# Causal attention with 16 heads: the probabilities are turned by VectorE in 32x32 blocks instead of by TensorE, the value product runs on 32x64 tiles, and the rope halves are swapped by transfers

## The chip, the cores and the metric

One NeuronCore of a Trainium2 chip runs the program. It has five engines with an instruction stream of their own: TensorE (PE in the rows; its weight loads are PEld), VectorE (DVE), ScalarE (ACT), GpSimd (POOL) and SyncE (SP), which here issues every transfer. They meet only in semaphores. The metric is the device time of one execution in microseconds.

## What is computed

A transformer layer for 4 sequences of 1024 tokens of width 256: layer norm, attention, residual, layer norm, a mixture of experts, residual. The change is in the attention.

```python
q = x @ Wqa @ Wqb                      # 16 heads of 128 + 64 (rope)
compressed, k_pe = split(x @ Wkva)     # 64 + 64
k_nope, v = split(compressed @ Wkvb)   # 128 + 128 for each head
scores = (q_nope @ k_nope.T + rope(q_pe) @ rope(k_pe).T) / sqrt(192)
attn = softmax(where(causal, scores, -max))
x = x + concat_heads(attn @ v) @ Wout
```

## The kernel before

The kernel works with absorbed weights: per head a query row of 128 numbers (64 rope, 64 against the latent) is multiplied with a key row of 128 numbers that all heads share, and the value of a key is its latent row of 64 numbers, in `v32`. Products that need accuracy are made of a high part and a low part (`qh`, `ql`, `kTh`, `kTl`, type fp32r) in three matmuls. The value product is plain fp32, which the trace shows as two loads and two matmuls for each.

`attention_prepare` (the first 70 us) makes keys, values and weights; `attention` runs 8 pairs of heads for each of 4 sequences, 32 pairs; `ffn` follows. The attention is a software pipeline: `run(r)` writes body r, from r = -1 to 32. Body 0 is the first with scores, bodies 1 to 31 are alike, and body 32 (`LAST`) holds only the end of pair 31 and the first steps of the router. The order inside a body is written out by hand in one list for each engine (`TENSOR`, `VECTOR`, `SCALAR`, `POOL`), with lists of their own for body 0 and body 32. In the names c is the half of the queries (0: tokens 0 to 511, 1: 512 to 1023), a the head of the pair, j the tile of 128 queries:

- `Q(c,a)`: queries of a half, two matmuls of 512 columns into a bank of PSUM. `ROT` on VectorE multiplies them with cosine (128 partitions) and, crosswise, with sine (two instructions of 32 partitions) into `rot1` and `rot2`; `ADD` on GpSimd adds; `HIGH` on ScalarE and `LOW` on GpSimd split the sum into `qh` and `ql`.
- `S(c,a,j)`: scores of 128 queries against 128(4c+j+1) keys. `MAX` on VectorE adds the mask and finds the maximum; `EXP` on ScalarE writes the probabilities and their sum. A pair has 16 of each, 9216 columns in all.
- `T(c,kb,a)`: the probabilities of key block kb are turned by TensorE, 128x128 for each query tile (line 1233; 72 for a pair), into three banks of PSUM. `OUT` copies them to `pT`, on ScalarE (line 1318) or VectorE (line 1382).
- `PV(c,first,count)`: value product, `v32` (128 keys x 64) against `pT`, the two heads in the two column halves of the array, 128x64 tiles; three of them for a pair: (1,0,4), (1,4,4), (0,0,4), with 48 matmul records in all.
- `INV`: reciprocals of the row sums; SyncE stores them (line 1107) and reads them back spread over partitions (line 1111) into `linv_b`. `O` on VectorE scales the product with them (line 1400); `OHIGH` (ScalarE) and `OLOW` (GpSimd) split it; `Y` multiplies with the output weights; `ACC` adds into `acc`, which starts as x and is stored per half after 8 pairs.

GpSimd also splits the first expert weights near the end (`split_first_quad`).

## Time and profile before

| | us |
|---|---|
| median of 3 runs | 1732.66 (1731.46 to 1732.78) |
| profiled execution | 1732.48, of which span 1730.7 |
| prepare and body 0 | to about 105 |
| bodies 1 to 31 | 31 of 35.53 each |
| body 32 | 1206.7 to 1238.9 |
| experts | from 1238.9 to the end |

A view by stretches gives busy time of each engine; a list of groups gives the mean length of an instruction, which for TensorE is longer than the distance to the next one, since its matmuls are pipelined. What a matmul costs is therefore read from the starts in the view by time.

### The profile page before, as it was taken

The numbers are of one execution on the slowest core, as the hardware profiler recorded it, in microseconds if no ns is written. First come the engines' busy times: TensorE is split into PE (matmuls) and PEld (weight loads), VectorE is DVE, ScalarE is ACT, GpSimd is POOL, SyncE is SP. The second block draws the span as 40 slices with busy tenths as digits, with TensorE's granted clock in tenths as the row PEclk, the third lists the DMA queues.
The fourth block names the chain that finished last, engine by engine and source line by source line (L and its number), as shares of the span: only waits on it lengthen the run. The fifth ranks groups of instructions, "written<-read, shape, count | busy, mean of one in ns | idle before, by whom it ended". The sixth has DMA issues, their size and how long they took to land.

```text
span 1730.7 us, 31809 instructions
## 1 busy us (share of the span) xinstructions
PE 1662.5 (96%) x11024; PEld 1357.5 (78%) x11024; DVE 1248.5 (72%) x2923; ACT 955.1 (55%) x2255; POOL 509.9 (29%) x433
## 2 busy tenths in 40 slices
PE   5799999999999999999999999999999999999998
PEld 4667777777777777777777777777699999999998
DVE  6888888888888788888888888888654554555543
ACT  6566666666666666666666666666433333433332
POOL 4543334323333333423343333335310110110100
PEclk9899999999999999999999999999999999999999
DMA  8300010012000003000002210001300000000000
GB/s 287 117 26 20 20 32 25 20 47 96 20 25 20 20 32 111 26 20 26 25 26 65 65 32 24 22 19 38 110 1 25 26 1 25 26 14 12 13 13 13
DMA packets 50204, 68.49 MB, mean 40 GB/s; under 512 B 8512, under 2 KB 33088, under 8 KB 50048
## 3 DMA queue, kind: packets, MB, share of 16 engines
q1 hardware_dynamic: 50048, 66.45, 11.6%
q8 instruction: 93, 1.52, 0.4%
q14 instruction: 63, 0.52, 0.1%
HBM read 52.00 MB, written 14.42 MB: 38 GB/s over the span
## 4 chain that ended last, share of the span: by engine, by line
PE 81%; issue 8%; DVE 4%; ACT 2%; DMA 1%; POOL 1%; ACTq 0%; DVEq 0%
PE aps L43 46%; PE fps L43 23%; PE aps L1233 9%; PE fps L1618 2%; ACT probs L1307 1%; DVE f_stats L739 1%; DMA raw_down<-in_down 1%; DVE nmax L1357 0%; POOL rot L1454 0%; PE fps L700 0%; PE fps L668 0%; DVE aTl L1759 0%; DVE rot L1371 0%; DVE aps L1357 0%; DVE rot L792 0%
## 5 line engine op out<-in xcount | busy, mean ns | idle before, releaser
L1307 ACT ACTIVATE probs<-aps,nmax 128x384 f32<-128x384 f32 (+7 forms) x512 | 378.6, 743 | 229.7 <-DVE nmax L1357 224.0
L1357 DVE CUSTOM_DVE_ANT_0 aps<-aps,mask_row 128x384 f32<-128x384 f32 (+7 forms) x512 | 387.2, 772 | 105.9 <-PE aps L43 100.3
L1233 PE MATMUL aps<-ident,probs 128*128 128x128 f32 x2304 | 324.0, 272 | 0.9 <-ACT probs L1307 0.6
L43 PE MATMUL aps<-kTh,qh 128*128 128x512 f32 (+3 forms) x768 | 293.3, 382 | 23.3 <-ACT probs L1307 18.4
L1233 PEld LDWEIGHTS aps<-ident,probs 128*128 128x128 f32 x2304 | 271.7, 140 | 27.2 <-issue 1.5
L1318 ACT COPY pT<-aps 128x512 f32<-128x512 f32 (+3 forms) x485 | 229.5, 504 | 92.1 <-PE aps L1233 89.5
L43 PE MATMUL aps<-pT,v 128*64 128x512 f32 (+3 forms) x1536 | 268.9, 492 | 0.6 <-ACT pT L1318 0.6
L43 PE MATMUL aps<-kTl,qh 128*128 128x512 f32 (+3 forms) x768 | 257.9, 343 | 0.0
L1454 POOL TENSOR_TENSOR rot<-rot 64x512 f32<-64x512 f32 x128 | 163.9, 1280 | 211.8 <-DVE rot L1371 211.8
L43 PE MATMUL aps<-kTh,ql 128*128 128x512 f32 (+3 forms) x768 | 221.8, 343 | 0.0
L43 PEld LDWEIGHTS aps<-pT,v 128*64 128x64 f32 x1536 | 101.7, 136 | 152.1 <-issue 142.1
L1461 POOL TENSOR_TENSOR ql<-rot,qh 128x512 fp32r<-128x512 f32 x128 | 164.9, 1288 | 158.5 <-ACT qh L1299 158.5
L43 PEld LDWEIGHTS aps<-kTh,qh 128*128 128x128 f32 x768 | 145.7, 190 | 74.4 <-issue 57.9
L1468 POOL TENSOR_TENSOR ol<-o,oh 128x512 fp32r<-128x512 f32 x64 | 82.3, 1286 | 352.8 <-ACT oh L1325 352.8
L1702 ACT CAST aTh<-fps 128x512 fp32r<-128x512 f32 (+1 forms) x96 | 52.9, 552 | 236.1 <-PE fps L1618 236.0
L1759 DVE TENSOR_TENSOR aTl<-fps,aTh 128x512 fp32r<-128x512 f32 (+1 forms) x96 | 62.0, 647 | 167.3 <-ACT aTh L1702 167.3
L43 PE MATMUL fps<-wth,qh 128*128 128x352 f32 x512 | 176.1, 344 | 2.0 <-PEq L833 2.0
L1371 DVE TENSOR_TENSOR rot<-aps,sinT 32x512 f32<-32x512 f32 x256 | 174.2, 680 | 3.5
L43 PE MATMUL fps<-wtl,qh 128*128 128x352 f32 x512 | 166.3, 325 | 0.0
L43 PE MATMUL fps<-wth,ql 128*128 128x352 f32 x512 | 166.2, 325 | 0.0
L43 PEld LDWEIGHTS aps<-kTl,qh 128*128 128x128 f32 x768 | 146.7, 191 | 9.5
L43 PEld LDWEIGHTS aps<-kTh,ql 128*128 128x128 f32 x768 | 136.7, 190 | 8.2
(190 smaller groups left out, 2878.1 us busy)
## 6 DMA issues: line engine op xcount, KB each, us to landing
linv_b<-inverses_scratch SPq DMA_DIRECT2D x128, 128.0 KB, 2.8
wqs<-wq_scratch SPq DMA_DIRECT2D x30, 256.0 KB, 3.1
raw_numbers<-in_x SPq DMA_DIRECT2D x8, 512.0 KB, 6.2
acc<-in_x SPq DMA_DIRECT2D x8, 512.0 KB, 4.0
inverses_scratch<-linv_t SPq DMA_DIRECT2D x256, 1.0 KB
x_scratch<-acc SPq DMA_DIRECT2D x8, 512.0 KB, 2.9
x<-x_scratch SPq DMA_DIRECT2D x8, 512.0 KB, 3.9
out<-x SPq DMA_DIRECT2D x7, 512.0 KB, 2.9
```

The lines of the kernel that those rows point to most:

```text
L43: return nc.tensor.matmul(out, lhsT, rhs, start=start, stop=stop, skip_group_check=True)
L1233: last = nc.tensor.transpose(tps[:, TS.index(x) % 3, j * P:(j + 1) * P], probs[c][:, c * (pair % 2), a, off:off + P], t.ident[:])
L1307: nc.scalar.activation(probs[c][:, c * (r % 2), a, off:off + w], sps[:, at:at + w], ACT.Exp, bias=nmax[:, c, a, j:j + 1], scale=-1.0, accu ...
L1318: nc.scalar.copy(pT[:, k % PT_BUFS, s:QC], tps[:, k % 3, s:QC]).then_inc(t_sb["scalar"], 1)
L1357: nc.vector.tensor_tensor_reduce(out=s, in0=s, in1=mask[:, N - PW[c][j]:N], scale=-1.0, scalar=3.0e38, op0=ALU.add, op1=ALU.min, accum_out ...
L1371: last = nc.vector.tensor_tensor(rot2[to:to + 32, k, :], sps[source:source + 32, at:at + QC], t.sinT[to:to + 32, cols], ALU.mult)
L1454: nc.gpsimd.tensor_tensor(rot1[0:64, k, :], rot1[0:64, k, :], rot2[:, k, :], ALU.add).then_inc(q_add, 1)
L1461: nc.gpsimd.tensor_tensor(ql[:, a, cols], rot1[:, k, :], qh[:, a, cols].bitcast(F32), ALU.subtract).then_inc(q_split, 1)
L1468: nc.gpsimd.tensor_tensor(ol[:, cols], o32[:, c, :], oh[:, cols].bitcast(F32), ALU.subtract).then_inc(o_low, 1)
L1618: last = nc.tensor.transpose(turned_in(i, q)[:, (m - 4 * q) * P:(m - 4 * q + 1) * P], act_sb[:, i % 2, m * P:(m + 1) * P], t.ident[:])
L1702: nc.scalar.copy(aTh[:, i % 2, m.start:m.stop, :].rearrange("p m n -> p (m n)"), turned_in(i, q)[:, 0:len(m) * P]).then_inc(aT_h, 1)
L1759: nc.vector.tensor_tensor(aTl[:, i % 2, m.start:m.stop, :].rearrange("p m n -> p (m n)"), turned_in(i, q)[:, 0:len(m) * P], aTh[:, i % 2, ...
```

## The change

- `T` and `OUT` go. `TURN(c,a,j)` on VectorE turns the whole probability row block of one `EXP` in blocks of 32x32, SBUF to SBUF: on partitions 32a' to 32a'+31 lie then, for each block b of 32 keys, the probabilities of those keys for the queries 32a' to 32a'+31 of every query tile. There are 16 for a pair, 128 to 1024 columns wide, one for each `EXP`. `EXP` writes into a ring of 5 rows, so it waits for the `TURN` of 5 rows before.
- The value product contracts 32 keys at a time: for each block b, each row group a' and each head a matmul of 32 rows x 64 columns, at most 128 columns moving, into banks 4 to 7 (one for each row group). A pair has 244 + 116 = 360 of them, with two passes each 720 records in the place of 48. They are written as six pieces of eight key blocks. Values lie four times over partitions in `vrep`, loaded by SyncE in pieces of 256 bytes.
- `ROT` on VectorE becomes: `RAW`, one copy of PSUM to `rot1` by ScalarE; `SWAP`, two transfers of 32 partitions that swap the halves into `rot2`; and three instructions on GpSimd, sine product, cosine product, sum.
- `acc` is double, loaded and stored for a whole sequence at once. `vrep` of sequences 0 and 1 is loaded at the end of body 0. Storing and spreading the inverses are two jobs of SyncE's list. The first expert weights are split by ScalarE and VectorE in body 32.
- All order lists and bank numbers are new.

```diff
-                    for j in range(t_cols(x) // P, 4):
-                        last = nc.tensor.transpose(tps[:, TS.index(x) % 3, j * P:(j + 1) * P],
-                                                   probs[c][:, c * (pair % 2), a, off:off + P], t.ident[:])
-                            last = mm(nc, ops[64 * a:64 * a + 64, s:QC], t.v32[:, pair // PAIRS % 2, kb, :],
-                                      pT[:, k % PT_BUFS, s:QC], kb == 0, kb == KB[c] - 1)
+                    if part == 0:
...
+                        pe.wait_ge(p_turned, last_of("tr", c, pair))
+                        banks_free(x)
+                    n = BLOCKS[c] // PARTS[c]
+                    for b in range(part * n, (part + 1) * n):
+                        for a in range(4):
+                            s = max(0, b // 4 - 4 * c) * S32
+                            if b // 4 >= 4 * c and b % 4 > a:
+                                s += S32
+                            if s == 4 * S32:
+                                continue
+                            for h in range(2):
+                                last = mm(nc, banks[64 * h:64 * h + 64, OB + a, s:4 * S32],
+                                          vrep[32 * a:32 * a + 32, pair // PAIRS % 2, b, :],
+                                          pT[c][32 * a:32 * a + 32, h, b, s:], b == 0, b == BLOCKS[c] - 1)
...
+                def turn_job(x):
+                    dve.wait_ge(e_done, count(EXP(c, a, j), r))
+                    if r > 0:
+                        dve.wait_ge(pv_done, last_of("p", c, r - 1))
+                    nc.vector.transpose(pT[c][:, a, 0:w // S32, j * S32:(j + 1) * S32],
+                                        probs[:, SLOT[EXP(c, a, j), r], 0:w].rearrange("p (b k) -> p b k", k=S32))\
+                        .then_inc(p_turned, 1)
...
-                    nc.vector.tensor_tensor(rot1[:, k, :], sps[:, at:at + QC], t.cosT[:, cols], ALU.mult)
-                    for to, source in ((0, 32), (32, 0)):
-                        last = nc.vector.tensor_tensor(rot2[to:to + 32, k, :], sps[source:source + 32, at:at + QC],
-                                                       t.sinT[to:to + 32, cols], ALU.mult)
+                    nc.scalar.copy(rot1[:, rot_slot(x, r), :], banks[:, bank_of(Q(c, a), r), :]).then_inc(q_raw, 1)
...
+                sp.dma_start(rot2[0:32, k, :], rot1[32:64, k, :]).then_inc(q_swapped[k], 16)
+                sp.dma_start(rot2[32:64, k, :], rot1[0:32, k, :]).then_inc(q_swapped[k], 16)
...
+                    nc.gpsimd.tensor_tensor(rot2[:, k, :], rot2[:, k, :], t.sinT[:, cols], ALU.mult).then_inc(q_turned, 1)
+                    nc.gpsimd.tensor_tensor(rot1[0:64, k, :], rot1[0:64, k, :], t.cosT[0:64, cols], ALU.mult)\
+                        .then_inc(q_turned, 1)
+                    pool.wait_ge(q_turned, 2 * n)
                     nc.gpsimd.tensor_tensor(rot1[0:64, k, :], rot1[0:64, k, :], rot2[:, k, :], ALU.add).then_inc(q_add, 1)
```

TensorE, in a body of the middle, the second half of the value product of c = 1 before (`PV(1,4,4)`, a piece between scores and transposes):

```order
L1233 MATMUL aps<-ident,probs 128x128 x2
L43 MATMUL aps<-pT,v 64x512 [waits pT_by_vector_in_sbuf,pT_by_scalar_in_sbuf]
L43 MATMUL aps<-pT,v 64x512
L43 MATMUL aps<-pT,v 64x384 x2
L43 MATMUL aps<-pT,v 64x256 x2
L43 MATMUL aps<-pT,v 64x128 x2
L43 MATMUL aps<-kTh,qh 128x384 [waits exp_done,q_split]
```

and after, the last of its four pieces (`PV(1,3)`), with the output product that follows:

```order
L46 MATMUL aps<-pT_second,vrep 64x64 x8
L46 MATMUL aps<-pT_second,vrep 64x32 x2
L46 MATMUL aps<-pT_second,vrep 64x64 x6
L46 MATMUL aps<-pT_second,vrep 64x32 x4
L46 MATMUL aps<-pT_second,vrep 64x64 x4
L46 MATMUL aps<-pT_second,vrep 64x32 x6
L46 MATMUL aps<-pT_second,vrep 64x64 x2
L46 MATMUL aps<-pT_second,vrep 64x32 x20
L46 MATMUL aps<-w2h,oh 128x256 [waits exp_done,o_low]
```

One matmul of the list is a load and a matmul for each of two passes. The transposes between the pieces are gone, and each piece is many short matmuls.

VectorE, the middle of a body, before (the four `ROT` of a pair stand between the maxima):

```order
L1369 TENSOR_TENSOR rot<-aps,cosT 128x512 [waits q_split,q_ps]
L1371 TENSOR_TENSOR rot<-aps,sinT 32x512 x2
L1357 ISA aps,nmax<-aps,mask_row 128x896 [waits scores_ready]
L1357 ISA nmax 128x1
L1369 TENSOR_TENSOR rot<-aps,cosT 128x512 [waits q_split,q_ps]
L1371 TENSOR_TENSOR rot<-aps,sinT 32x512 x2
L1382 COPY pT<-aps 128x384 [waits pv_done,pT_ready]
L1382 COPY pT<-aps 128x256 [waits pv_done,pT_ready]
```

and after, where `O(1)` opens the turns of the second half:

```order
L1406 STREAM_TRANSPOSE pT_first<-probs 128x8x32 [waits pv_done,exp_done]
L1428 TENSOR_TENSOR o32<-aps,linv_b 128x4x4x32 [waits o_low,inverses_1_in_sbuf,pv_done]
L1406 STREAM_TRANSPOSE pT_second<-probs 128x28x32 [waits pv_done,exp_done]
L1440 TENSOR_TENSOR acc<-aps,acc 128x512 [waits y_ps,x_even_loaded]
L1396 ISA aps,nmax<-aps,mask_row 128x896 [waits scores_ready]
L1396 ISA nmax 128x1
L1396 ISA aps,nmax<-aps,mask_row 128x768 [waits scores_ready]
```

The turn reads `probs` and no PSUM, and stands behind `O(1)` because both need the value product of the pair before to be done.

SyncE, a body of the middle, before:

```order
L1114 DMA wqs<-wq_scratch 128x512 [waits q_ps]
L1107 DMA inverses_scratch<-linv_t 8x32 [waits inverses_turned,o_in_sbuf]
L1107 DMA inverses_scratch<-linv_t 8x32 x3
L1111 DMA linv_b<-inverses_scratch 64x512 [waits inverses_0_kept]
L1111 DMA linv_b<-inverses_scratch 64x512
```

and after:

```order
L1146 DMA wqs<-wq_scratch 128x512 [waits q_ps]
L1142 DMA rot<-rot 32x512 [waits q_raw]
L1143 DMA rot<-rot 32x512
L1130 DMA inverses_scratch<-linv_t 8x32 [waits inverses_turned,o_in_sbuf]
L1130 DMA inverses_scratch<-linv_t 8x32 x3
L1142 DMA rot<-rot 32x512 [waits q_raw]
L1143 DMA rot<-rot 32x512
L1137 DMA linv_b<-inverses_scratch 64x512 [waits inverses_1_kept]
```

The swap of the second head's queries now stands behind the wait for the inverses of the pair.

## Rows read from the trace of the kernel before

**Rows 1.** The page: busy time, share of the span and instructions of each engine.

```profile
PE 1662.5 (96%) x11024; PEld 1357.5 (78%) x11024; DVE 1248.5 (72%) x2923; ACT 955.1 (55%) x2255; POOL 509.9 (29%) x433
```

**Rows 2.** Stretches: length, busy of PE, PEld, DVE, ACT, POOL, PEclk, DMA; a middle body, body 32.

```profile
595.32:630.85 35.53, 34.77 (x224) 26.69 (x225) 29.18 (x64) 22.66 (x54) 12.76 (x10) 1.00 0.07 24
1206.70:1238.90 32.20, 28.71 (x212) 21.63 (x210) 21.84 (x58) 15.70 (x31) 16.98 (x14) 0.95 0.41 133
```

**Rows 3.** Chain of waits in order of time: start, length, what (eight transposes).

```profile
567.32 0.87 PE aps L1233 x8
```

**Rows 4.** PE by time (start, length, instruction): both shapes of value product and what follows.

```profile
587.66 2.37 PE L43 MATMUL aps<-pT,v 128*64 128x512 f32 x16
589.97 0.44 PE L43 MATMUL aps<-kTh,qh 128*128 128x384 f32 x1
...
1215.66 3.65 PE L43 MATMUL aps<-pT,v 128*64 128x512 f32 x16
1219.24 1.95 PE L1233 MATMUL aps<-ident,probs 128*128 128x128 f32 x15
```

**Rows 5.** PE by time, the router and mask products on 32-row and 32-column tiles.

```profile
1238.87 0.43 PE L43 MATMUL fps<-mw,xq 32*128 32x352 f32 x4
1239.23 0.50 PE L43 MATMUL fps<-wth,mu 128*32 128x352 f32 x4
...
1240.44 0.78 PE L43 MATMUL fps<-wth,mu 128*32 128x352 f32 x8
1241.03 0.78 PE L43 MATMUL fps<-wtl,mu 128*32 128x352 f32 x8
```

**Rows 6.** DMA queues: the one that carries TensorE's instructions.

```profile
q8 instruction: 93, 1.52, 0.4%
```

**Rows 7.** DVE groups: instruction, out<-in, shapes, count, busy, mean ns, idle before.

```profile
L1371 DVE TENSOR_TENSOR rot<-aps,sinT 32x512 f32<-32x512 f32 x256 | 174.2, 680 | 3.5
L1369 DVE TENSOR_TENSOR rot<-aps,cosT 128x512 f32<-128x512 f32 x128 | 87.0, 680 | 10.1 <-PE aps L43 8.5 <-POOL ql L1461 1.3 <-issue 0.2
L789 DVE COPY rot<-soft_h 128x512 f32<-128x512 f32 x8 | 3.4, 427 | 0.3
```

**Rows 8.** Tile pT: its copies by VectorE, ns shortest, median, longest.

```profile
L1382 DVE COPY pT<-aps x283: 280/552/691, 90.2 to 1201.7; 128x256 f32<-128x256 f32 x49, 128x384 f32<-128x384 f32 x45, 128x512 f32<-128x512 f32 x33, 128x128 f32<-128x128 f32 x15
```

**Rows 9.** DVE by time: a 32x32 turn, the maximum behind it, and two maxima.

```profile
579.24 0.21 DVE L1392 STREAM_TRANSPOSE linv_t<-linv 128x32 f32<-128x32 f32 x1
579.38 0.65 DVE L1369 TENSOR_TENSOR rot<-aps,cosT 128x512 f32<-128x512 f32 x1
...
586.55 1.23 DVE L1357 CUSTOM_DVE_ANT_0 aps<-aps,mask_row 128x1024 f32<-128x1024 f32 x1
587.70 0.14 DVE L1357 DVE_READ_ACCUMULATOR2_ANT nmax<- 128x1 f32 x1
```

**Rows 10.** ACT and POOL groups: copies of the turned blocks, rope sum, low part.

```profile
L1318 ACT COPY pT<-aps 128x512 f32<-128x512 f32 (+3 forms) x485 | 229.5, 504 | 92.1 <-PE aps L1233 89.5
L1454 POOL TENSOR_TENSOR rot<-rot 64x512 f32<-64x512 f32 x128 | 163.9, 1280 | 211.8 <-DVE rot L1371 211.8
L1461 POOL TENSOR_TENSOR ql<-rot,qh 128x512 fp32r<-128x512 f32 x128 | 164.9, 1288 | 158.5 <-ACT qh L1299 158.5
```

**Rows 11.** POOL by time: the low part waits for the high part.

```profile
575.07 1.28 POOL L1461 TENSOR_TENSOR ql<-rot,qh 128x512 fp32r<-128x512 f32 x1 [0.73 <-ACT qh L1299]
```

**Rows 12.** DMA issues: out<-in, count, KB each, us from issue to landing.

```profile
linv_b<-inverses_scratch SPq DMA_DIRECT2D x128, 128.0 KB, 2.8
v<-values_scratch SPq DMA_DIRECT2D x2, 256.0 KB, 7.1
```

**Rows 13.** PE by time at the start; the chain of waits at the end of body 32.

```profile
77.55 0.69 PE L43 MATMUL aps<-kTh,qh 128*128 128x384 f32 x1 [4.22 <-POOL ql L1461]
...
1230.70 3.17 DMA x_scratch<-acc
1233.89 8.80 DMA raw_down<-in_down
```

More of the change, by code:

```diff
@@ new lines, in attention @@
+        SCALAR = [RAW(1, 0), RAW(1, 1), EXP(0, 0, 0), EXP(0, 0, 3), EXP(0, 0, 1), EXP(0, 1, 3), HIGH(1, 0),
+                  EXP(0, 1, 0), EXP(0, 0, 2), EXP(0, 1, 2), EXP(0, 1, 1), RAW(0, 0), EXP(1, 0, 0), HIGH(1, 1),
+                  EXP(1, 0, 2), OHIGH(1), RAW(0, 1), EXP(1, 1, 2), EXP(1, 0, 1), EXP(1, 1, 0), HIGH(0, 0),
+                  EXP(1, 0, 3), EXP(1, 1, 1), HIGH(0, 1), EXP(1, 1, 3), OHIGH(0)]
+        POOL = [ROT(1, 0), LOW(1, 0), ROT(1, 1), LOW(1, 1), ROT(0, 0), OLOW(1), LOW(0, 0), ROT(0, 1), LOW(0, 1),
+                OLOW(0)]
@@ new lines, in attention, with of @@
+        SS = [x for x in TENSOR if x[0] == "s"]
+        COUNT, KINDS = {}, {}
+        for bodies in (tensor_body, vector_body, scalar_body, pool_body, sync_body):
+            for r in BODIES:
+                for x in bodies(r):
+                    if x[0] not in ("router", "mask", "stats", "quad"):
+                        KINDS[x[0]] = KINDS.get(x[0], 0) + 1
+                        COUNT[x, r] = KINDS[x[0]]
+        def count(x, r):
+            return COUNT[x, r]
+        def of(kind, x):
+            return (kind,) + x[1:]
@@ L1295, in high_job @@
                     pair = r + age(x)
[L1296 removed]
+                    act.wait_ge(q_add, count(ROT(c, a), r))
                     if pair > 0:
[L1298 to L1299 removed]
+                        act.wait_ge(s_ready, max(at_pair(y, pair - 1) for y in SS if y[1:3] == (c, a)))
```

603 lines of the change are left out of this document (293 added, 310 removed).

## The prediction

> **What bounds the kernel now.** I read the page first: TensorE is busy 96% of the span, VectorE 72% [rows 1]. Then one body of the middle, since 31 equal bodies of 35.53 us make 1101 of the 1730.7 us: there TensorE is busy 34.77 us, VectorE 29.18, ScalarE 22.66, GpSimd 12.76 [rows 2]. TensorE leaves 0.76 us free, so a pair costs what TensorE's list costs. The question is what the list costs after the change, and which other list is then the longest.
>
> **TensorE, what goes.** Eight transposes take 0.87 us on the chain, 0.109 each [rows 3]; 72 for a pair make 7.8 us. The value products go in their old form: two pieces of the narrowing kind (512, 384, 256 and 128 columns) take 589.97 - 587.66 = 2.31 us each, the piece with 512 columns throughout 1219.24 - 1215.66 = 3.58 [rows 4], together 8.2. What stays (scores, queries, output product, small gaps) is 34.77 - 7.8 - 8.2 = 18.8 us.
>
> **TensorE, what comes.** From the two pieces the rate of today: 2 passes of 1280 columns take 2.31 us, 2 passes of 2048 take 3.58; the difference, 1536 column passes in 1.27 us, is 0.83 ns each, and 0.18 us is left over per piece for entering and leaving the tiled form. A pair streams 4608 columns for each row group (the fourth row group has the most), at two passes 9216 x 0.83 = 7.7 us if all eight tiles (four row groups, two column halves) run side by side. Where only 32 columns move, the load of 64 weight columns is longer: a load of 128 columns is hidden in 0.109 us [rows 3], so I take 0.055 for 64 against 0.027 for the stream, 16 times, 0.4 us. Six pieces at 0.18 make 1.1. Sum 9.2 us. TensorE's new list: 18.8 + 9.2 = 28.0 us.
>
> Do eight tiles run side by side? The row-tiled form is in the trace: four matmuls of 32 rows and 352 columns begin together and the next instruction starts 1239.23 - 1238.87 = 0.36 us later, their loads, the stream and a change of form included [rows 5]. One after the other, four streams of 352 columns at the 0.83 ns of fp32 or even half of that would take 0.58 us or more without the loads. Column tiles too: eight matmuls of 352 columns in four column tiles follow each other in 0.59 us [rows 5], that is 0.295 for four, the same 0.83 ns a column. The two together are not in the trace, nor is a stretch with so many starts. Bound from below: 9.2. From above: today's narrowest value matmuls start two in every 0.109 us; if no faster rate of starts existed, 720 x 0.055 = 39 us. I take 9.2, because within a group of four the starts cost nothing that the 0.36 us leave room for.
>
> The Trainium skill, "TensorEngine Tiling (Array Packing)", Performance Considerations, Instruction Overhead, speaks against the change: it gives each matmul about 60 cycles of overhead and warns against tiling a dimension that is small already. At 2.4 GHz that is 25 ns, and 720 of them are an estimate of 18 us instead of 9.2 by that page. The four starts in rows 5 don't bear it out as a cost in series. It would lead to the second rival.
>
> TensorE's instructions come in packets: 93 of them for the 11,024 matmuls, as many loads [rows 1] and the waits between, some 250 instructions each; they take 0.4% of 16 engines' 1730.7 us, 1.2 us each [rows 6]. A body will have about 1700 instructions, 6.6 packets, 8 us in 30. I cost it at nothing; its cover is the work before a piece, and without it one packet, 1.2 us, would show in each piece of 256 instructions, 7 us a pair.
>
> **VectorE.** `ROT` goes: (174.2 + 87.0) / 32 = 8.2 us a pair [rows 7]. Its copies go: 283 of about 0.5 us, 4.4 us a pair [rows 8]. 29.2 - 8.2 - 4.4 = 16.6 us stay (maxima, sums, scaling, inverses). 16 turns of 9216 columns come. A turn of 32 columns lasts 0.21 us and the next instruction starts after 0.14 [rows 9]. VectorE's rate elsewhere is near 1.04 ns a column: the maximum of 1024 columns gives way after 1.15 us [rows 9]. Wide turns are not in the trace. From below: at the rate of the copy inside SBUF, 427 ns for 512 columns [rows 7], 9216 x 0.83 = 7.7 us. From above: if all of the 0.21 us for 32 columns beyond the 0.14 of spacing were per-column work, 2.2 ns, 20 us. I take 1.04 ns and 0.15 us an instruction, 9.6 + 2.4 = 12.0, since 32 columns at 1.04 ns leave 0.11 to 0.18 us of fixed cost, as everywhere on this engine. VectorE's new list: 28.6 us, now the longest by a little.
>
> **ScalarE** loses 229.5 / 32 = 7.2 us of copies and gains four of about 0.59, 2.4 [rows 10]: 17.9 us, no bound. **GpSimd**: for each of four query tiles three instructions of 1.28 and one of 1.29, and `OLOW` twice 1.29: 23.1 us [rows 10]; `LOW` waits 0.73 us for `HIGH` [rows 11], 2.9 for four, 26.0 in all. It starts after `RAW` (0.6) and a swap; the nearest transfer lands in 2.8 us [rows 12]. The first chain in a body is 0.5 + 0.6 + 2.8 + 3.8 + 0.7 + 1.3 = 9.7 us, and TensorE reaches the first scores of the second half after some 9 us of other work. The second swap waits in SyncE's queue behind the wait for the inverses, whose instruction on VectorE comes after about 4 us; GpSimd is then still busy with the first until 9.7. So the wait is hidden; uncovered it would cost 2.8 us a pair.
>
> **Period.** Three lists of 28.6 (VectorE), 28.0 (TensorE) and 26.0 us (GpSimd). The first piece of the value product waits for all turns of its half, and these turns wait for the last piece of the pair before: about 16 us of VectorE (eight turns of 8.3, six maxima, the sums) and 11 us of TensorE (6.9 of pieces, 4.3 of scores and queries between) in turn, 27 us, inside 28.6. Today the bound engine leaves 0.76 us; with a second list as long I take 1.2: 29.8 us. 31 x (35.53 - 29.8) = 178 us saved.
>
> **Ends.** Body 0 waits for GpSimd today (4.22 us once [rows 13]) and will wait for its three instructions and the swap; the values are loaded only at its end, 7.1 us for such a load [rows 12]. Nothing to 10 us, I take +5. Body 32 (32.2 us) loses 52 transposes, 5.7 us, but VectorE gets 3.7 us of weight splitting ahead of `O(1)`, and the store before the load of the expert weights doubles from 512 KB in 3.17 us [rows 13]: from -5 to +4, I take 0. The experts are untouched. Sum on the profiled execution: span 1730.7 - 178 + 5 = 1558, and 1.8 around it, 1560. The runs' median is 0.2 us from the profiled execution.
>
> **Rivals.**
> 1. The queries bound a body. For: GpSimd's 26.0 us are close, and two of the four swaps stand behind waits in SyncE's list. If both are uncovered with their `RAW`, 26.0 + 2 x 3.4 = 32.8, with gaps 33.2 us: 1730.7 - 72 + 5 + 1.8 = 1665. Against: two slots of `rot1` let a swap run while GpSimd works on the other.
> 2. Slower: the eight tiles take turns. If the row groups go in two turns, the pieces cost 16.2 + 1.1 us, TensorE's list is 36.1, the period 37.5: 1730.7 + 61 + 5 + 1.8 = 1799. It decides from 22 ns a matmul on (720 of them in 15.7 us, where TensorE's list reaches 35.5). For: no stretch of the trace has so many starts, and 39 us is the far bound. Against: rows 5. The page named above would give 18 us and a period near 39, about 1845.
> 3. Slower: turns at 2.1 ns a column, 21.6 us, VectorE's list 38.2, the period 39: 1845. Against: the 0.14 us spacing of the narrow turn. It decides from 19 us of turns on.
>
> **How the numbers follow.** The forecast (period 28.3 to 32, 1513 to 1630) has 0.68, rival 1 0.14, rival 2 0.11, rival 3 0.05, and 0.02 lie at no change. Predicted 1560. From 1495 (turns at the copy's rate, TensorE's list alone) to 1690 leaves out rivals 2 and 3. A difference of 0.2% is about what a measurement can tell from none; faster by more than that 0.82, within it 0.02, slower 0.16.
>
> **What would show it.** A middle body near 30 us with VectorE busy above 27; a 1024-wide turn giving way after about 1.2 us; a full piece of 128 matmuls in 1.9 us with eight starts within 0.06 us; the low part of the second half's queries done before TensorE asks. A piece above 2.8 us makes rival 2 true, a turn above 2 us rival 3, TensorE waiting for `ql` rival 1.

## The result

The changed kernel takes 1748.38 us (median of 6 runs, 1743.20 to 1754.92), the kernel before 1732.72 (6 runs, 1731.46 to 1733.13): 1.0094 times as long, with a 95% interval of 1.0069 to 1.0119. It is slower by 16 us where 173 us less were forecast (1560), and it lies outside the range of 1495 to 1690. Its runs also differ among themselves by 0.7%, those of before by 0.1%. The profiled execution took 1750.21 us, its span 1748.4.

The page of the profile after, answering to [rows 1] and [rows 6]: busy time of TensorE and VectorE, the granted clock in 40 slices, the queue that brings TensorE's instructions, the chain by engine.

```profile
PE 1564.5 (89%) x30224; PEld 1355.7 (78%) x30224; DVE 1185.9 (68%) x2772; ACT 810.9 (46%) x1902; POOL 819.2 (47%) x681
...
PEclk9889999998999999899999899999899999999999
...
q8 instruction: 240, 3.93, 0.9%
...
PE 70%; DVE 7%; issue 6%; DMA 5%; POOL 4%; ACT 2%; SPq 2%; DVEq 0%; ACTq 0%; POOLq 0%
```

TensorE is busy 98 us less than before, yet the span is 18 us longer: a gain is there and is given back as idle time. The packets of instructions went from 93 to 240. The chain has 6% "issue", time in which nothing that the profile shows was waited for. That share alone is no sign of anything new, since the chain of the kernel before has more of it:

```profile
PE 81%; issue 8%; DVE 4%; ACT 2%; DMA 1%; POOL 1%; ACTq 0%; DVEq 0%
```

What is new is a wait for issue in front of TensorE's matmuls, in the list of waits below.

Stretches from one first-half reciprocal of VectorE (L1416) to the next, one per body: length, busy of PE, PEld, DVE, ACT, POOL, PEclk, DMA. The first two are bodies of the middle, the third stands at the end of the first sequence, the last is the first body.

```profile
460.10:492.50 32.40, 30.59 (x844) 25.78 (x834) 26.98 (x60) 17.98 (x42) 20.55 (x17) 1.00 0.14 37
492.50:527.40 34.90, 30.97 (x844) 25.89 (x835) 27.27 (x60) 18.09 (x42) 23.89 (x20) 1.00 0.17 48
378.60:425.70 47.10, 32.97 (x794) 27.87 (x787) 27.37 (x59) 18.12 (x42) 22.52 (x19) 0.86 0.49 131
95.67:140.40 44.73, 30.82 (x652) 25.53 (x651) 26.30 (x58) 17.98 (x42) 20.97 (x18) 0.81 0.64 123
```

ScalarE does what was forecast (18 us), and VectorE is busy 27 us where its list was put at 28.6. TensorE leaves 1.8 us of the shorter body and 3.9 of the longer one idle, so no engine fills its body. From the times of the same reciprocals, the whole span:

| us | before | after | e5_spread_early | e6_spread_early_quarter |
|---|---|---|---|---|
| start to the first reciprocal | 89.8 | 95.7 | 96.3 | 96.3 |
| first body | 27.1 | 44.7 | 35.3 | 28.9 |
| three bodies at sequence ends | 35.5 each | 47.1, 47.3, 43.4 | 33.3, 33.9, 34.3 | 30.6, 29.9, 30.1 |
| the 27 others, mean | 35.55 | 34.09 | 33.77 | 30.22 |
| rest of the last body and experts | 547.4 | 549.8 | 550.6 | 545.0 |

The last two columns are experiments told below. Before, the 27 bodies lie between 35.5 and 35.8; after, between 31.2 and 37.7.

Three kinds of idle time stand behind this. First, TensorE by time: start, length, instruction, and in brackets the idle time before it. A whole piece of the value product, and one that stops after 108 of its 128 matmuls.

```profile
586.85 2.10 PE L46 MATMUL aps<-pT_second,vrep 32*64 32x128 f32 x128
588.88 0.33 PE L46 MATMUL aps<-kTh,qh 128*128 128x128 f32 x1
...
449.62 1.84 PE L46 MATMUL aps<-pT_second,vrep 32*64 32x128 f32 x108
452.91 0.65 PE L46 MATMUL aps<-pT_second,vrep 32*64 32x128 f32 x20 [1.45 <-issue]
```

The whole piece gives way after 588.88 - 586.85 = 2.03 us (forecast 1.9): eight tiles do run side by side. The other one waits in its middle, where no semaphore stands. Behind such a stop the granted clock can fall to the lower of its two levels:

```profile
562.43 1.44 PE L46 MATMUL aps<-pT_second,vrep 32*64 32x64 f32 x104
563.81 0.39 PE L46 MATMUL aps<-w2h,oh 128*128 128x256 f32 x1
...
574.86 0.43 PE L46 MATMUL aps<-pT_first,vrep 32*64 32x96 f32 x17 [2.24 <-issue]
...
577.03 2.15 PE L46 MATMUL aps<-pT_first,vrep 32*64 32x64 f32 x104
579.11 0.58 PE L46 MATMUL aps<-w2h,oh 128*128 128x256 f32 x1
```

The granted clock is 1.00 from 562.43 to 563.81 and 0.50 (1.2 GHz) from 576.6 to 583.2; two pieces of 104 matmuls give way after 1.38 and 2.08 us.

Second, SyncE at the end of the first sequence (start, time in which it issues, transfer), and GpSimd at the same place.

```profile
392.05 8.35 SPq L1156 DMA_DIRECT2D vrep<-values_scratch  x4
403.83 0.38 SPq L1211 DMA_DIRECT2D x_scratch<-acc  x1
408.41 0.39 SPq L1160 DMA_DIRECT2D acc<-in_x  x1
...
409.72 0.54 SPq L1142 DMA_DIRECT2D rot<-rot  x1
...
416.47 1.25 POOL L1488 TENSOR_TENSOR rot<-rot,sinT 64x512 f32<-64x512 f32 x1 [14.56 <-DMA rot<-rot]
```

The first swap of the next body is issued only after the residual is stored (403.83), has landed (408.41) and 1 MB for a later sequence is asked for; it lands behind that megabyte at 416.47. Third, the waits, total, times and longest:

```profile
PEld aps L46 <- issue: 203.8, 383, 3.4
POOL rot L1488 <- DMA rot<-rot: 192.1, 65, 16.9
...
PE aps L46 <- issue: 89.3, 85, 3.8
...
PE aps L46 <- POOL ql L1498: 35.2, 10, 10.6
...
PE aps L46 <- DMA vrep<-values_scratch: 10.0, 1, 10.0
```

TensorE's 10.0 us for the first values lie in the first body. The same view of the kernel before:

```profile
PEld aps L43 <- issue: 225.2, 714, 3.0
...
PE aps L43 <- issue: 0.6, 1, 0.6
```

Weight loads waited for issue as much before, and they overlap matmuls. The matmuls themselves waited 0.6 us before and wait 89.3 now, in 85 places.

### The profile page after: what moved, and what is told of

The parts are those of the page before. It is cut to its first block, busy times and chain, and to the rows that moved or that the text cites. A ratio compares the mean times of both kernels' runs of the same rounds, so it can differ in the third digit from the quotient of the medians.

```text
span 1748.4 us, 69212 instructions
## 1 busy us (share of the span) xinstructions
PE 1564.5 (89%) x30224; PEld 1355.7 (78%) x30224; DVE 1185.9 (68%) x2772; ACT 810.9 (46%) x1902; POOL 819.2 (47%) x681
## 3 DMA queue, kind: packets, MB, share of 16 engines
q1 hardware_dynamic: 82432, 87.44, 17.6%
## 4 chain that ended last, share of the span: by engine, by line
PE 70%; DVE 7%; issue 6%; DMA 5%; POOL 4%; ACT 2%; SPq 2%; DVEq 0%; ACTq 0%; POOLq 0%
PE aps L46 44%; PE fps L46 23%; DMA rot<-rot 3%; PE fps L1649 2%; DVE aps L1396 2%; DVE pT_second L1406 2%; POOL rot L1492 1%; POOL rot L1488 1%; DVE acc L1440 1%; POOL rot L1489 1%; POOL ql L1498 1%; DMA x_scratch<-acc 1%; ACT probs L1348 1%; SPq L1130 1%; SPq L1142 1%
## 5 line engine op out<-in xcount | busy, mean ns | idle before, releaser
L1348 ACT ACTIVATE probs<-aps,nmax 128x1024 f32<-128x1024 f32 (+7 forms) x512 | 375.8, 738 | 318.4 <-DVE nmax L1396 303.6
L1396 DVE CUSTOM_DVE_ANT_0 aps<-aps,mask_row 128x384 f32<-128x384 f32 (+7 forms) x512 | 379.7, 761 | 188.9 <-PE aps L46 187.4
L46 PE MATMUL aps<-kTh,qh 128*128 128x512 f32 (+3 forms) x768 | 286.4, 373 | 45.8 <-POOL ql L1498 35.2
L46 PEld LDWEIGHTS aps<-pT_second,vrep 32*64 32x64 f32 x15616 | 231.9, 134 | 82.2 <-issue 79.6
L46 PE MATMUL aps<-pT_second,vrep 32*64 32x128 f32 (+1 forms) x15616 | 266.3, 265 | 29.5 <-issue 28.2
L1406 DVE STREAM_TRANSPOSE pT_second<-probs 128x768 f32<-128x768 f32 (+3 forms) x256 | 258.6, 1030 | 1.4 <-ACT probs L1348 0.3
L1488 POOL TENSOR_TENSOR rot<-rot,sinT 64x512 f32<-64x512 f32 x128 | 162.9, 1273 | 192.1 <-DMA rot<-rot 192.1
L46 PE MATMUL aps<-pT_first,vrep 32*64 32x128 f32 (+3 forms) x7424 | 120.7, 249 | 52.7 <-issue 42.5
L46 PEld LDWEIGHTS aps<-pT_first,vrep 32*64 32x64 f32 x7424 | 105.8, 136 | 78.5 <-issue 68.1
L1337 ACT CAST qh<-rot 128x512 fp32r<-128x512 f32 x128 | 79.2, 619 | 183.9 <-POOL rot L1492 183.7
L1489 POOL TENSOR_TENSOR rot<-rot,cosT 64x512 f32<-64x512 f32 x128 | 163.4, 1276 | 0.0
L46 PEld LDWEIGHTS aps<-kTl,qh 128*128 128x128 f32 x768 | 148.3, 193 | 12.2 <-issue 1.7
```

Of the source, the lines that this page charges most:

```text
L46: return nc.tensor.matmul(out, lhsT, rhs, start=start, stop=stop, skip_group_check=True)
L1337: nc.scalar.copy(qh[:, a, c * QC:(c + 1) * QC], rot1[:, rot_slot(x, r), :]).then_inc(q_high, 1)
L1348: nc.scalar.activation(probs[:, SLOT[x, r], 0:w], sps[:, at:at + w], ACT.Exp, bias=nmax[:, c, a, j:j + 1], scale=-1.0, accum_out=lsum[:, c ...
L1396: nc.vector.tensor_tensor_reduce(out=s, in0=s, in1=mask[:, N - PW[c][j]:N], scale=-1.0, scalar=3.0e38, op0=ALU.add, op1=ALU.min, accum_out ...
L1406: nc.vector.transpose(pT[c][:, a, 0:w // S32, j * S32:(j + 1) * S32], probs[:, SLOT[EXP(c, a, j), r], 0:w].rearrange("p (b k) -> p b k", k ...
L1488: nc.gpsimd.tensor_tensor(rot2[:, k, :], rot2[:, k, :], t.sinT[:, cols], ALU.mult).then_inc(q_turned, 1)
```

## The experiments

The theory is that instruction supply, the order of SyncE's list at sequence ends, and the late load of the first values cost the gain, each by itself. The rival is the prediction's first: queries, swaps and GpSimd bound a body.

**e1_boundary.** The transfers of a sequence end go out one or two per body, between the last swap and `KEEP(0)`. With `n = r % 8`, `between` issues the keys at n = 0 to 2, the values at 3 to 6, the stores at 1 to 4 (256 KB each in place of one of 1 MB) and the loads of the residual at 6 and 7 (512 KB each). The router's and the first experts' loads are spread over the last sequence in the same way.

```diff
                 for x in sync_body(r):
+                    if 1 <= r < LAST and x == KEEP(0):
+                        between(r)
                     job[x[0]](x, r)
...
                     sp.dma_start(x2_v[b], acc[:, 1 - b % 2]).then_inc(x2_stored, 16)
-                    if b + 2 < B:
-                        sp.wait_ge(x2_stored, 16 * (b + 1))
-                        load_acc(b + 2)
```

> The order of SyncE's transfers at the three sequence ends alone is changed: keys (3 of 512 KB), values (4 of 256 KB), residual stores (4 of 256 KB) and loads (2 of 512 KB), the router's and the experts' loads go out one per body, behind the last swap of the body, in place of all at once ahead of the next body's first swap. Theory (queue order): bodies 8, 16 and 24, which took 47.1, 47.3 and 43.4 us beside 34.1 of the others, fall to the others' length: 1748.4 - 3 x 12 = 1712 (1705 to 1722). Rival (those bodies are long because of instruction supply or the clock): under 10 us less, 1740 to 1748.

Measured: 1699.84 us (1691.66 to 1705.78), ratio to before 0.9813 [0.9774, 0.9853]; 48 us less than the changed kernel and below the expected 1705 to 1722. The three bodies take 33.2, 32.7 and 34.4 us. The one at the end of the first sequence has its full clock again (0.86 in the changed kernel):

```profile
383.15:416.35 33.20, 30.78 (x806) 25.45 (x792) 27.22 (x59) 18.20 (x42) 19.90 (x17) 1.00 0.18 52
```

These three give 37.5 us (137.8 to 100.3); the others 9.7 (27 times 34.09 - 33.73). This version is faster than both kernels, and it leaves nothing out.

**e2_quarter.** The value product on tiles of 128 rows, a quarter of the instructions.

```diff
-                        for a in range(4):
...
-                            for h in range(2):
-                                last = mm(nc, banks[64 * h:64 * h + 64, OB + a, s:4 * S32],
-                                          vrep[32 * a:32 * a + 32, pair // PAIRS % 2, b, :],
-                                          pT[c][32 * a:32 * a + 32, h, b, s:], b == 0, b == BLOCKS[c] - 1)
+                        s = max(0, b // 4 - 4 * c) * S32
+                        for h in range(2):
+                            last = mm(nc, banks[64 * h:64 * h + 64, OB + b % 4, s:4 * S32],
+                                      vrep[:, pair // PAIRS % 2, b, :], pT[c][:, h, b, s:], b < 4, b >= BLOCKS[c] - 4)
```

> The value product on 128x64 tiles in place of 32x64: a piece has 32 matmuls and 32 weight loads in place of 128 and 128, and about the same columns streamed side by side. It leaves out the parting of the four query groups, so that the weighted values are mixed; everything else is as in the changed kernel. Theory (instruction supply): about 1.3 packets of 256 instructions a body go in place of 6.9 or so, no piece is broken, and a normal body falls from 34.1 to 30 to 31.5 us: 1748 - 27 x 3.1 = 1665 (1640 to 1690). Rival (queries, swaps and GpSimd set the body): the normal body stays at 33 to 34 us, 1720 to 1748.

Measured: 1631.62 us (1626.93 to 1635.50), 0.9421 [0.9402, 0.9441]. The 27 bodies fall from 34.09 to 30.27 us, inside the expected 30 to 31.5; the time is 8 us below the expected range. The sequence ends stay long (44.5, 45.0, 38.3). TensorE's matmuls have no wait for issue left in the attention. The rival is refuted as the main cause: neither queries nor GpSimd were touched.

**e4_noswap.** `SWAP` issues nothing, and GpSimd's first product reads `rot1[0:64]` in place of `rot2`.

```diff
-                sp.dma_start(rot2[0:32, k, :], rot1[32:64, k, :]).then_inc(q_swapped[k], 16)
-                sp.dma_start(rot2[32:64, k, :], rot1[0:32, k, :]).then_inc(q_swapped[k], 16)
```

> The swaps of the rope halves leave out their transfers: GpSimd multiplies the unswapped halves by the sines as soon as ScalarE has copied the queries, so that the queries are wrong; the number of GpSimd's instructions is the same. Rival (the chain ScalarE copy, swap, GpSimd, ql sets the body): each chain is some 3 to 4 us shorter, TensorE's waits for ql (77 us in all) go, 1748 to 1680 or less. Theory (instruction supply and queue order): only what the swap lost behind the transfers at three sequence ends comes back, about 7 us each, 1720 to 1740.

Measured: 1691.56 us (1688.80 to 1692.18), 0.9766 [0.9751, 0.9780], between the two expectations. Sequence ends take 38.7, 40.3 and 39.1, so 20 us of the 57 are theirs; the 27 bodies take 32.85 in place of 34.09, another 33. The rival holds in part; e9 and e10 return to it.

**e6_fine.** The second half's value product in eight pieces of four key blocks, one between every two score or query tiles.

```diff
-PARTS = [2, 4]
+PARTS = [2, 8]
...
-        TENSOR = [Q(1, 0), Q(1, 1), S(0, 0, 2), S(0, 0, 0), S(0, 0, 3), Y(0, 0), S(0, 0, 1), S(0, 1, 3), PV(1, 0),
+        TENSOR = [Q(1, 0), Q(1, 1), S(0, 0, 2), S(0, 0, 0), S(0, 0, 3), Y(0, 0), S(0, 0, 1), PV(1, 0), S(0, 1, 3),
+                  PV(1, 1), S(0, 1, 0), PV(1, 2), S(0, 1, 1), PV(1, 3), S(0, 1, 2), PV(1, 4), S(1, 0, 0), PV(1, 5), Q(0, 0),
+                  PV(1, 6), S(1, 0, 2), PV(1, 7), Q(0, 1), Y(0, 1), S(1, 1, 2), S(1, 0, 1), S(1, 1, 0), S(1, 0, 3),
```

> The value product of the second half in eight pieces of four key blocks (128 instructions each), one between every two score or query tiles, in place of four pieces of eight key blocks (256 instructions); the number of instructions is unchanged and so is every other engine's order. Theory (instruction supply): 6.9 packets of 3.4 us are 23.5 us of a body of 34.1, so they suffice if the instructions are asked for evenly; the four pieces of the second half no longer run out, and a body falls by 1 to 2 us: 1695 to 1725. Rival (the pieces break for another reason, or the query chain sets the body): within 8 us of 1748.

Measured: 1780.59 us (1779.38 to 1782.17), 1.0286 [1.0269, 1.0303], 32 us slower than the changed kernel: a miss. The matmuls' waits for issue fell only from 89.3 to 61.8 us and those of the weight loads rose from 203.8 to 243.4, while VectorE and ScalarE wait longer for scores that now come later:

```profile
PEld aps L46 <- issue: 243.4, 545, 3.6
...
ACT probs L1348 <- DVE nmax L1396: 421.0, 319, 11.2
DVE aps L1396 <- PE aps L46: 275.2, 125, 14.8
```

In the changed kernel the last two are 303.6 and 187.4. The run moved two things at once and doesn't decide between them.

**m1_supply.** TensorE alone. `small(64)` is 64 products on 32x64 tiles with 128 columns, that is 128 loads and 128 matmuls; `long` is products on 128x128 with 512 columns.

```diff
+            for _ in range(12):
+                small(64)
+            long(96)
```

> TensorE alone, with nothing to wait for: 12 pieces of 256 instructions (64 products on 32x64 tiles, 128 columns) in a row; then 10 pieces each followed by 14, 10 or 6 long products (128x128, 512 columns); then 20 half pieces each followed by 7 or 3 long ones. It computes nothing of the reference. Theory (instructions arrive at one packet of 256 per 3.4 us at best): the 12 pieces take 12 x 3.4 = 41 us though one takes 1.7 us uninterrupted; 14 long ones (3.1 us) behind a piece cover it, 4.8 us a round; 6 long ones (1.3 us) don't, 3.6 us a round in place of 3.0; a half piece with 7 long ones isn't held (2.4 us a round), with 3 it is (1.8 in place of 1.5). Rival (the pieces broke because the fetches shared the DMA engines with other transfers, of which there are none here): the 12 pieces take 20 to 22 us and no round is longer than its products.

Measured, TensorE by time, the start of the 12 pieces, the end, a round with six long products, and a half piece with three:

```profile
34.28 3.84 PE L46 MATMUL aps<-x,w 32*64 32x128 f32 x255
39.27 2.08 PE L46 MATMUL aps<-x,w 32*64 32x128 f32 x128 [1.15 <-issue]
42.73 2.08 PE L46 MATMUL aps<-x,w 32*64 32x128 f32 x128 [1.38 <-issue]
...
75.46 0.32 PE L46 MATMUL aps<-x,w 32*64 32x128 f32 x1 [1.37 <-issue]
75.71 22.07 PE L46 MATMUL aps<-xl,wl 128*128 128x512 f32 x96
...
226.05 2.10 PE L46 MATMUL aps<-x,w 32*64 32x128 f32 x128
...
229.66 2.16 PE L46 MATMUL aps<-x,w 32*64 32x128 f32 x128
...
352.61 1.21 PE L46 MATMUL aps<-x,w 32*64 32x128 f32 x64
...
354.64 1.21 PE L46 MATMUL aps<-x,w 32*64 32x128 f32 x64
```

The 12 pieces take 75.71 - 34.28 = 41.4 us, 3.45 each, where their work is 2.03; there are no other transfers. After the first 510 instructions TensorE mostly stops after every 128 matmuls and 128 loads. From that first stop on a piece takes (75.46 - 39.27) / 10 = 3.62 us; the step from 39.27 to 42.73, 3.46 us, is the fastest that repeats. Supply is shown as a limit by itself, at about 13.5 to 14 ns an instruction. The granted clock was at its lower level for 10 of these 41 us, which makes the pieces there longer, but the steps of 3.46 us stand at the full clock. Rounds with 14 and with 10 long products ran without a stop, as did half pieces with seven. The shorter rounds were forecast badly: six long products behind a piece made a round of 3.6 us by their own length, with one stop in ten rounds (268 instructions at 13.4 ns each, just at the limit), and the half pieces with three (2.03 us a round of 134 instructions, 15 ns each) ran without a stop, since they asked for no more than that rate.

The Trainium skill, "Runtime: NRT & Kernel Launch", Instruction fetch mechanics, says that instructions arrive in blocks of 256, the next block while the current one runs, and that crossing a block is mostly hidden. The 256 agree with the packets (70 for the 17,898 loads and matmuls of this run); the last does not hold where 256 instructions run in 2.03 us. The first stop after 510 instructions fits the two blocks in hand of which a note in that section speaks, not the 2048 instructions that the section gives TensorE.

**e3_half.** Both heads' columns in one product on 32x64 tiles, even and odd key blocks on the two halves of the array: half the instructions.

```diff
-                            for h in range(2):
-                                last = mm(nc, banks[64 * h:64 * h + 64, OB + a, s:4 * S32],
...
-                                          pT[c][32 * a:32 * a + 32, h, b, s:], b == 0, b == BLOCKS[c] - 1)
+                            g = b % 2
...
+                            last = mm(nc, banks[64 * g:64 * g + 64, OB + a, 2 * s:8 * S32].rearrange("p (h t) -> p h t", h=2),
+                                      vrep[32 * a:32 * a + 32, pair // PAIRS % 2, b, :],
+                                      pT[c][32 * a:32 * a + 32, :, b, s:], b < 2, b >= BLOCKS[c] - 2)
```

> The value product on 32x64 tiles with both heads' 128 columns in one product of 256 columns, even key blocks on one half of the array and odd ones on the other: half the instructions (128 in place of 256 a piece), about the same columns side by side. It leaves out adding the two halves, so that the output is of no use; everything else is as in the changed kernel. Theory (instruction supply): 3.5 to 4 packets a body in place of 6.9; almost no piece is broken, and the time is near that of the quarter (1631.6): 1635 to 1660. Rival (the small tiles themselves are slow, and the quarter won by its 128-row tiles): above 1700.

Measured: 1633.90 us (1630.68 to 1635.23), 0.9431 [0.9417, 0.9445], the quarter's time within 2.3 us, with 150 packets in place of 108 and 240. So it is the number of instructions and not the 32-row tiles, and half of them is already few enough: the matmuls' waits for issue are 2.1 us.

**e5_spread_early.** e1_boundary, with `load_values(0)` ahead of body 0's swaps and the second sequence's loads in bodies 3 and 4. The lines are against e1_boundary.

```diff
-                if r == 0:
+                if r == -1:
                     sp.wait_ge(t.values_stored, 32)
-                    for b in (0, 1):
-                        load_values(b)
-                        load_acc(b)
+                    load_values(0)
```

> The changed kernel with the sequence transfers one per body, as in e1_boundary, and the first sequence's values loaded ahead of the first body's swaps (they are stored at 70 us and were asked for at 107); the second's values and residual go out in bodies 3 and 4. Theory (queue order): the first body's 10.0 us wait for the values goes as well: 1699.8 - 10 = 1690 (1684 to 1697). Rival (TensorE has something else to wait for there): 1697 to 1702.

Measured: 1700.12 us (1697.33 to 1706.07), 0.9820 [0.9801, 0.9840]. In the profiled executions the first body falls from 43.9 to 35.3 us and the span from 1703.7 to 1695.5, but the medians of the two versions, from runs that spread over 9 and 14 us, don't show it: inconclusive for the time.

**e6_spread_early_quarter.** e5_spread_early and the quarter together, both edits as above.

> e5_spread_early with the value product on 128x64 tiles (a quarter of its instructions; the parting of the four query groups is left out, so that the weighted values are mixed). Theory (queue order, first values and instruction supply are three costs that add up): in e2_quarter the three bodies at sequence ends took 44.5, 45.0 and 38.3 us beside 30; without that excess of 38 us and the first wait of 10 us, 1631.6 - 48 = 1584 (1575 to 1592), and every body near 30 us. Rival (one stall hid the other): above 1600.

Measured: 1577.75 us (1577.06 to 1578.37), 0.9108 [0.9093, 0.9123]. The costs add up: 1700.12 - 1577.75 = 122 us hang on the number of instructions, and the 53.9 us less than e2_quarter on the order of the transfers and the first values. Its output is of no use, so it measures what the costs are worth and is no kernel that could replace the other. The first body falls from 42.6 to 28.9 us, the scatter of the runs is gone (0.1%), and the bodies are level. One of the middle, and one at a sequence end:

```profile
305.86:335.92 30.06, 29.34 (x302) 24.12 (x300) 26.84 (x60) 17.79 (x42) 23.12 (x20) 1.00 0.17 46
366.49:396.33 29.84, 29.28 (x302) 24.10 (x300) 26.72 (x59) 17.79 (x42) 21.51 (x18) 1.00 0.24 66
```

Not all of the 122 us are stops. The same full piece as at 586.85, with a quarter of the instructions:

```profile
327.72 1.97 PE L46 MATMUL aps<-pT_second,vrep 128*64 128x128 f32 x32
329.62 0.33 PE L46 MATMUL aps<-kTh,qh 128*128 128x128 f32 x1
```

It gives way after 1.90 us in place of 2.03, and the pieces with narrower products save more (1.05 in place of 1.38). By the medians of the unbroken pieces at full clock, the six of a pair take 10.7 us on the 32x64 tiles and 9.3 in the quarter. That is some 40 of the 122 us for 32 pairs, an estimate from these lengths. The matmuls' waits for issue are 77.2 us in e5_spread_early and none here; how much of these and of the lower clock behind them shows in the time was not separated.

**e7_even, e8_even_less.** e5_spread_early with TensorE's order alone changed. e7 moves score tiles, queries and output products; e8 moves two output products. e7:

```diff
-        TENSOR = [Q(1, 0), Q(1, 1), S(0, 0, 2), S(0, 0, 0), S(0, 0, 3), Y(0, 0), S(0, 0, 1), S(0, 1, 3), PV(1, 0),
-                  S(0, 1, 0), S(0, 1, 1), S(0, 1, 2), PV(1, 1), S(1, 0, 0), Q(0, 0), PV(1, 2), S(1, 0, 2), Q(0, 1),
-                  PV(1, 3), Y(0, 1), S(1, 1, 2), S(1, 0, 1), S(1, 1, 0), S(1, 0, 3), S(1, 1, 1), PV(0, 0), S(1, 1, 3),
-                  PV(0, 1), Y(1, 1), Y(1, 0)]
+        TENSOR = [Q(1, 0), Q(1, 1), S(0, 0, 2), S(0, 0, 0), S(0, 0, 3), Y(0, 0), S(0, 0, 1), PV(1, 0), S(0, 1, 3),
+                  S(0, 1, 0), S(0, 1, 1), S(0, 1, 2), PV(1, 1), Q(0, 0), S(1, 0, 0), S(1, 0, 2), PV(1, 2), Q(0, 1), Y(0, 1),
+                  S(1, 0, 1), PV(1, 3), S(1, 1, 2), S(1, 1, 0), S(1, 0, 3), S(1, 1, 1), PV(0, 0), S(1, 1, 3), Y(1, 1),
+                  PV(0, 1), Y(1, 0)]
```

> e5_spread_early with TensorE's order of a body changed so that more other work stands between two pieces of 256 instructions: some 1.6 us behind the first of the second half (was 1.0), 2.3 behind the second (1.2), 2.0 behind the third (1.6), 1.9 behind the first of the first half (1.3). Other engines' orders and all counts are unchanged. Theory (a fetch of 256 instructions costs 3.45 us and is only asked for when the one before it has arrived, so that each run of 256 instructions must last 3.45 us by itself): pieces of 1.7 us with 1.8 us behind them fit, the breaks in pieces (43 over 0.5 us, 54 us in all) fall to less than half, a normal body from 33.8 to 31.5 to 33, 1625 to 1675. Rival (scores that come later hold up VectorE and ScalarE, as in e6_fine): 1695 to 1730.

> As e7_even but only two products of the attention's output are moved: one ahead of the fourth piece of the second half, one between the two pieces of the first half. No score is moved. Theory: two of the four short distances grow by 0.6 us each, 1680 to 1697. Rival (distances don't matter): 1697 to 1703.

Measured: e7 1841.21 us (1838.08 to 1855.81), 1.0647 [1.0620, 1.0674]; e8 1701.94 (1694.46 to 1711.07), 0.9832 [0.9804, 0.9859], no change against e5_spread_early. e7 is a miss by far, outside both of its expectations. In it TensorE waits for exponentials whose banks it needs sooner, and VectorE for value products that come later:

```profile
DVE o L1449 <- PE aps L46: 202.0, 63, 7.3
PE aps L46 <- ACT probs L1369: 119.8, 109, 3.3
```

In e5_spread_early the first is 38.2 and the second 4.2. In e8 the matmuls' waits for issue fell from 77.2 to 56.9 us and VectorE's wait for value products rose from 38.2 to 65.1, so a stop that is taken away does not give its length back by itself. Whether a better spacing could hide the supply is left open; in the two orders tried, moving scores cost more than it brought.

**e9_noswap, e10_shadow.** e5_spread_early without the swaps, and with transfers of the same shape that no engine reads or waits for; SyncE alone sees to it that the last one into the same slot has landed (the line with the plus stands in e10 alone).

```diff
-                sp.dma_start(rot2[0:32, k, :], rot1[32:64, k, :]).then_inc(q_swapped[k], 16)
+                sp.dma_start(shadow[0:32, k, :], t.cosT[32:64, 0:QC]).then_inc(q_swapped[k], 16)
```

> e5_spread_early without the transfers of the rope halves (GpSimd takes the unswapped halves at once, the queries are wrong). Theory (the queries' chain costs the rest of a normal body by itself, 34.09 to 32.85 in e4_noswap): 1700 - 31 x 1.0 = 1665 to 1680. Rival (the swap cost only behind the transfers at sequence ends, which are spread here): 1693 to 1702.

> As e9_noswap, but transfers of the same size and shape still go out at the same places, from a table into a buffer that nobody reads, and nobody waits for them. It tells the traffic from the wait. Theory (the wait for the swap costs, not its traffic): within 4 us of e9_noswap. Rival (the swaps' 64 KB get in the way of the instruction fetches on the same DMA engines): near e5_spread_early, 1693 to 1702.

Measured: e9 1673.10 us (1668.48 to 1677.92), 0.9662 [0.9646, 0.9678]; e10 1690.09 (1683.65 to 1693.51), 0.9756 [0.9740, 0.9771]. Of the 27 us, 17 come back with the traffic alone and 10 hang on the wait. The intervals of e9 and e10 don't meet; those of e10 and e5 do not either, with 0.3% between them. e10 lies between its two expectations, nearer the second.

**m2_traffic.** m1's row of 12 pieces three times: alone, beside swaps, beside 1 MB loads.

```diff
+            for n in range(12):
+                sp.dma_start(to[0:32, 0, :], xl[32:64, :].bitcast(F32)).then_inc(moved, 16)
+                sp.dma_start(to[32:64, 0, :], xl[0:32, :].bitcast(F32)).then_inc(moved, 16)
+                sp.wait_ge(moved, 32 * (n + 1))
...
+            for n in range(5):
+                sp.dma_start(big[:], ins["x"].rearrange("b (t p) d -> b p t d", p=P)[n % 4]).then_inc(moved, 16)
```

> TensorE alone as in m1_supply: three times 12 pieces of 256 instructions in a row, each behind 97 long products. Beside the first nothing moves; beside the second swaps of the rope's shape go out (two of 32x2048 bytes) one after the other; beside the third loads of 1 MB one after the other. It computes nothing of the reference. Theory (fetches share the DMA engines with the transfers): 41.4 us the first time, 43 to 48 beside the swaps, 60 or more beside the 1 MB loads. Rival (fetches are not held by other transfers): 41 to 42 three times.

Measured, TensorE by time, start and end of the three rows of pieces:

```profile
34.89 3.85 PE L46 MATMUL aps<-x,w 32*64 32x128 f32 x254
...
77.41 22.28 PE L46 MATMUL aps<-xl,wl 128*128 128x512 f32 x97
99.62 2.51 PE L46 MATMUL aps<-x,w 32*64 32x128 f32 x157
...
145.86 23.26 PE L46 MATMUL aps<-xl,wl 128*128 128x512 f32 x97
169.05 2.95 PE L46 MATMUL aps<-x,w 32*64 32x128 f32 x188
...
208.18 3.72 PE L46 MATMUL aps<-x,w 32*64 32x128 f32 x128 [4.92 <-issue]
...
223.63 22.28 PE L46 MATMUL aps<-xl,wl 128*128 128x512 f32 x97
```

42.5 us alone, 46.2 beside the swaps, 54.6 beside the loads (which ran for 25 of them, with single stops up to 4.92 us). The stops in the three rows come to 14.7, 17.9 and 22.8 us. The rest of the differences goes with the granted clock, 0.92, 0.91 and 0.81 in the three rows. So transfers do lengthen the supply, the loads less than expected. It is a way in which traffic can cost time that nobody waits for. That it is what cost the 17 us of e10 is not shown: its matmuls wait 73.8 us for issue, those of e9 67.2, and the other 10 us were traced to no wait.

**e11_by_scalar.** e5_spread_early with the swap as two copies by ScalarE.

```diff
+                    nc.scalar.copy(rot2[0:32, k, :], banks[32:64, bank, :])
+                    nc.scalar.copy(rot2[32:64, k, :], banks[0:32, bank, :])
+                    nc.scalar.copy(rot1[:, k, :], banks[:, bank, :]).then_inc(q_raw, 1)
```

> e5_spread_early with the two swaps of a rope half made by ScalarE, which copies 32 rows of the queries from PSUM twice more (32x512, about 0.6 us each by the 0.585 us of its 128x512 copy, 4.7 us a body) in place of the two transfers. Theory (the traffic and the latency of the swaps cost 17 and 10 us, and ScalarE, 18 of 33.8 us busy, has room): 1673 to 1688. Rival (ScalarE's longer turn delays the exponentials or the query banks come free later): 1695 to 1715.

Measured: 1704.35 us (1699.12 to 1715.43), 0.9858 [0.9829, 0.9886], no gain over 0.9820 [0.9801, 0.9840]. ScalarE's busy time grows by 150 us, 4.7 a pair, and what the missing transfers give back is used up; which wait takes it was not isolated.

## Why the prediction was wrong

- **What it had right.** VectorE's turns (1.04 ns a column and 0.15 us) are 1221 ns for 1024 columns and 308 for 128, the measured slope 1.02 ns:

```profile
L1406 DVE STREAM_TRANSPOSE pT_second<-probs 128x1024 f32<-128x1024 f32 x64 | 78.2, 1221 | 0.0
L1406 DVE STREAM_TRANSPOSE pT_first<-probs 128x128 f32<-128x128 f32 x64 | 19.7, 308 | 33.6 <-ACT probs L1348 33.4
```

  The 391 us of all turns are 12.2 a pair (forecast 12.0); rival 3 is refuted. The eight tiles run together, a whole piece in 2.03 us (1.9), so rival 2 is refuted. The Trainium skill, "TensorEngine Tiling (Array Packing)", Performance Considerations, Instruction Overhead, gives about 60 cycles a matmul, and for tiles of this size the trace does not agree: 128 matmuls in 2.03 us are 16 ns each.
- **What was luck.** With the causes taken away the 31 periods average 30.2 us against 29.8, and the kernel takes 1577.75 against 1560. Part of this nearness is luck. It was reached with a quarter of the instructions, whose pieces take 9.3 us a pair; those of the forecast kernel take 10.7 even unbroken, against the 9.2 of the sum. And the engine that fills the body is TensorE, busy 29.3 us (28.0 in the sum), not VectorE, busy 26.8 (28.6): two errors of opposite sign.
- **The step that failed: packets "I cost it at nothing".** The text had the count right (6.6 a body) and the size of one, and even a price if uncovered (7 us a pair). It took the work before a piece as cover, because it asked whether 6.6 packets of 1.2 us fit into 30 us on the DMA engines. The question was how fast one can follow another: 3.45 us alone (m1_supply), so that a piece of 256 instructions in 2.03 us outruns them whatever the mean. Price: 34.09 - 30.22 = 3.9 us a body for the 27 bodies, 122 us on e5_spread_early, of which by the estimate above some 40 are the pieces' own length and the rest goes with the stops and the clock behind them.
- **The step that was not taken: the moved swap against SyncE's list at a sequence end.** The list of waits ahead of a swap was read for a body of the middle, where the text costed the wait for the inverses. At three ends the same queue holds a store, its landing and 1 MB loads. Before, nothing that TensorE needed soon came through that queue; the change made every body's queries depend on it. They cost 13, 13 and 9 us over the mean of the other bodies, and all in all 48 us came back when they were spread (e1_boundary).
- **First body.** "I take +5" for body 0 and its values, with 10 as the upper bound: the start to the first reciprocal grew by 5.8, and the first body by 17.6, of which the wait for the values is 10.0. The chain of the first queries and the load of the values were two different waits and should have been added.
- **The last body** was taken at 0 (-5 to +4): from its last reciprocal to the end 527.0 in place of 523.2 us, and 1.4 less ahead of it, +2.4.
- **Rival 1** (queries bound a body, 0.14) named a real wait of the wrong size: swaps cost 27 us on e5_spread_early, 10 of them by waiting. By the sign that the text named, TensorE waiting for `ql`, it was there for 35.2 us in the changed kernel and 11.2 in e5_spread_early, most of it at a few places.
- **One period for all bodies.** The sum multiplied one body by 31. Before, this was safe since one full engine set the pace (35.5 to 35.8). After, no engine fills its body, and stops fall inside the pieces at changing places; behind some of them the granted clock is at its lower level for 3 to 7 us. Over the span it is 0.964, before 0.996, in e6_spread_early_quarter 0.989. What the clock alone costs was not separated.

## What to carry to other kernels

Count instructions as a resource with a rate: where TensorE's list asks for 256 of them in less than some 3.5 us, and does so for more than the 510 or so that it had in hand here, it stops, even if the average over a stage leaves room. When a transfer is put into the path of every step, read its whole queue, also at the rare places, and spread there what is not urgent: that alone made this change a gain of 1.9% instead of a loss of 0.9%. And take out one suspected cost at a time and then all together; only the last run showed that the costs add up and that nothing large is missing.
